# Attention scores as 64-row products in the two halves of the matmul array

## The reference, cut to what matters

```python
Qr = jnp.einsum('bnhd,dr->bnhr', Q, WQr)
Kr = jnp.einsum('bnhd,dr->bnhr', K, WKr)
scores = jnp.einsum('bnhr,bmhr->bnhm', Qr, Kr) / math.sqrt(RANK)   # RANK = 16
A = jax.nn.softmax(scores, axis=-1)
out = jnp.einsum('bnhm,bmhv->bnhv', A, V).reshape(b, n, d)
```

## Time and profile before

| | |
|---|---|
| median of 3 runs | 3451.5 us (3451.04 to 3457.17) |
| profiled execution | 3445.68 us, its span 3443.9 us |
| attention, from its first row tile to the last normalise | 175.1 to 1740.3 us of the span |
| PE busy over the span | 2747.7 us (80%) |
| DVE busy | 2382.6 us (69%) |
| ACT busy | 1604.9 us (47%) |
| row tiles (L678), column tiles (L689), value products (L704) | 2048, 2048, 4096 matmuls |
| maxima on DVE (L608), exponentials on ACT (L594) | 2048 of each |

### The profile page before, as it was taken

The page is one execution under the profiler, slowest core; times in us unless marked ns, Lnnn a source line. Parts: engine busy times, 40 slices in busy tenths (PEclk is TensorE's granted clock), DMA queues, the critical chain, the costliest instruction groups (busy, mean ns, idle before and its releaser), DMA issues. The chain is left out here.

```text
span 3443.9 us, 53771 instructions
## 1 busy us (share of the span) xinstructions
PE 2747.7 (80%) x13598; PEld 1256.8 (36%) x13598; DVE 2382.6 (69%) x4106; ACT 1604.9 (47%) x3030; POOL 1066.2 (31%) x1044
## 2 busy tenths in 40 slices
PE   3899999999999999999974977733367676587772
PEld 2423232332323223333253576621122222446662
DVE  2798888888888888888527912124499998793223
ACT  1327676776767667677731311113444444122110
POOL 1500000000000000000020577752399996036772
PEclk9969999999999999999985989866699989589996
DMA  8400000000000000000002078721133332125887
GB/s 283 134 20 20 21 20 11 20 20 20 20 11 20 20 20 20 11 20 20 1 8 86 23 190 205 197 63 41 41 117 107 102 110 64 47 64 136 214 216 199
DMA packets 184546, 255.14 MB, mean 74 GB/s; under 512 B 26256, under 2 KB 139984, under 8 KB 184272
## 3 DMA queue, kind: packets, MB, share of 16 engines
q1 hardware_dynamic: 140576, 195.81, 18.6%
q0 software_dynamic: 24576, 37.77, 6.2%
q10 hardware_dynamic: 19120, 18.40, 1.6%
HBM read 189.53 MB, written 62.03 MB: 73 GB/s over the span
## 5 line engine op out<-in xcount | busy, mean ns | idle before, releaser
L608 DVE TENSOR_REDUCE att_mx<-att_pR 128x1 f32<-128x512 f32 x2048 | 1271.0, 683 | 196.3 <-PE att_pR L678 193.4
L594 ACT ACTIVATE att_probs<-att_pS 128x512 f32<-128x512 f32 x2048 | 1062.9, 604 | 502.4 <-PE att_pS L689 502.2
L678 PE MATMUL att_pR<-att_ks,att_qs 96*128 96x512 bf16 x2048 | 801.3, 392 | 15.3 <-POOL att_vh L556 14.0
L689 PE MATMUL att_pS<-att_qs,att_ks 98*128 98x512 bf16 x2048 | 781.4, 385 | 26.2 <-issue 20.1
L704 PE MATMUL att_pA<-att_probs,att_vh 128*17 128x512 f32 x4096 | 544.2, 603 | 0.3 <-ACT att_acc_sb L582 0.2
L561 POOL COPY att_vh<-all_v 128x256 f32 (+1 forms) x32 | 12.7, 400 | 1423.3 <-PE att_pA L704 1423.3
L689 PEld LDWEIGHTS att_pS<-att_qs,att_ks 98*128 98x128 bf16 x2048 | 199.2, 98 | 645.1 <-ACT att_probs L594 405.1
L2019 PE MATMUL sc_pY<-sc_hc,all_ident 128*128 128x512 f32 x512 | 275.6, 665 | 121.5 <-DVE sc_hc L1976 104.9
L1903 POOL TENSOR_TENSOR sc_bh<-ssm_du,sc_b 128x1024 f32<-128x1024 f32 x128 | 298.5, 2353 | 15.9 <-DVE sc_hc L1976 10.2
L678 PEld LDWEIGHTS att_pR<-att_ks,att_qs 96*128 96x128 bf16 x2048 | 201.1, 98 | 278.2 <-DVE att_mx L608 140.2
L1966 DVE TENSOR_TENSOR_SCAN sc_bh<-sc_pD,sc_carry,sc_bh 128x512 f32<-128x512 f32 x192 | 232.2, 1260 | 0.0
(11 more groups left out here) (291 smaller groups left out, 3481.3 us busy)
## 6 DMA issues: line engine op xcount, KB each, us to landing
sc_b<-scan_rows SPq DMA_DIRECT2D x128, 256.0 KB, 3.3
expert_sum<-qkv_zeros ACTq DMA_DIRECT2D x4, 4224.0 KB, 28.2
att_qs<-query_parts SPq DMA_DIRECT2D x192, 64.0 KB, 2.1
att_ks<-key_parts SPq DMA_DIRECT2D x192, 64.0 KB, 2.1
f1e_wg<-in_w_gate SPq DMA_DIRECT2D x64, 192.0 KB
f1e_wu<-in_w_up SPq DMA_DIRECT2D x64, 192.0 KB
f1e_wd<-in_w_down SPq DMA_DIRECT2D x64, 192.0 KB
f2e_wg<-in_w_gate SPq DMA_DIRECT2D x64, 192.0 KB
```

Source lines behind the costliest of these rows:

```text
L594: act.activation(probs[:, k % (2 * HALF), :], pS[:, (s + k) % 3, :], ACT.Exp, scale=float(DK) ** -0.5).then_inc(expd, 1)
L608: dve.tensor_reduce(mx4[s][:, k // QC, k % QC:k % QC + 1], pR[:, (s + k) % 3, :], AX.X, ALU.max).then_inc(maxed, 1)
L678: pe.matmul(pR[:, (s + k) % 3, :], qs[s][0:PAIR_ROWS, t * P:(t + 1) * P], ks[s][0:PAIR_ROWS, c * GROUP:(c + 1) * GROUP], start=True, stop= ...
L689: pe.matmul(pS[:, (s + k) % 3, :], ks[s][:, t * P:(t + 1) * P], qs[s][:, c * GROUP:(c + 1) * GROUP], start=True, stop=True).then_inc(col_s ...
```

## The change

All score matmuls now have at most 64 rows, so that they fit in one half (upper 64 or lower 64 rows) of the array.

- The order of the six parts is changed, so that the first 64 rows hold the four products of parts 0 and 1. Row tiles are computed from those alone: the maxima come from two-part scores. The shift only has to be near the true maximum, since it cancels in the division.
- Every row of `qs` and `ks` gets a twin in the other half, in new tiles `q2` and `k2`. Even tiles use the upper half, odd tiles the lower half.
- A column tile is two products into one bank: 64 rows, then the remaining 34 (32 parts and the two shift rows).
- PE's order goes in pairs of steps: column tiles k and k+1 (upper, lower, upper, lower), then row tiles k and k+1. After every second pair there is a half of `values`.
- `pS` has four banks in place of three; the fourth is `pO`'s. `combine` and `turn_maxima` now borrow a place of the ring at step 56 of each head, and the places are numbered so that the ring comes out even. The next user of that place is column tile 59; it waits for `normalise` and `send`.
- `normalise` moves on DVE from the middle of the next head to behind `send`, at that same place.
- SP loads 24 pieces in place of 12 per head and issues four shift DMAs in place of two. POOL sets three more pairs of rows of ones.
- `pR` keeps its three banks, and a row tile k still waits for the maximum of tile k-3.

```diff
-Q_PARTS = (0, 1, 2, 0, 1, 0)
-K_PARTS = (0, 0, 0, 1, 1, 2)
+Q_PARTS = (0, 1, 0, 1, 2, 0)
+K_PARTS = (0, 0, 1, 1, 0, 2)
+MAX_PARTS = 4
+MAX_ROWS = DK * MAX_PARTS
...
+REST_ROWS = ROWS - MAX_ROWS
...
-    LOADS = 2 * len(Q_PARTS)
+    LOADS = 2 * 2 * len(Q_PARTS)
+    SHIFTS = 2 * SHIFT_ROWS
+    RING = 4
+    SIDE = STEPS - HALF
+    LEFT_OUT = (16, 32, 44)
+    PLACES = STEPS + 1 + len(LEFT_OUT)
...
-        pS = m.ps("pS", [P, 3, BANK])
+        pS = m.ps("pS", [P, RING, BANK])
         pA = m.ps("pA", [P, BANK])
-        pO = m.ps("pO", [P, BANK])
...
+        def place(k):
+            return k + sum(k >= left for left in LEFT_OUT) + (k >= SIDE)
+        SIDE_PLACE = place(SIDE) - 1
+        STEP_AT = {place(k): k for k in range(STEPS)}
+        def bank(at):
+            return pS[:, at % RING, :]
...
                     for r, part in enumerate(sel):
                         sp.dma_start(tile[DK * r:DK * r + DK, :],
                                      side[part, bass.ds(v(n * DK), DK), :]).then_inc(qk_in[s], 16)
+                        at = (DK * r + MAX_ROWS) % P
+                        sp.dma_start(twin[at:at + DK, :],
+                                     side[part, bass.ds(v(n * DK), DK), :]).then_inc(qk_in[s], 16)
...
                 pool.memset(ks[s][PAIR_ROWS:ROWS, :], 1.0).then_inc(consts, 1)
-                pool.wait_ge(consts, 8 + 2 * s)
+                pool.wait_ge(consts, 8 + 3 * s)
+                pool.memset(k2[s][PAIR_ROWS - MAX_ROWS:REST_ROWS, :], 1.0).then_inc(consts, 1)
+                pool.wait_ge(consts, 9 + 3 * s)
                 pool.memset(vh[s][:, :, DK:DK + 1], 1.0).then_inc(consts, 1)
...
             def head(n, s, turn, ahead):      # on DVE
                 if ahead >= 1:
-                    maxima(n + 1, s1, range(LEAD, 2 * LEAD))
-                if not start(n):
-                    normalise(n - 1)
-                if ahead >= 1:
-                    maxima(n + 1, s1, range(2 * LEAD, STEPS))
+                    maxima(n + 1, s1, range(LEAD, STEPS))
                     negate(n + 1, s1)
                 if ahead >= 2:
                     maxima(n + 2, s2, range(LEAD // 2))
                 if ahead >= 1:
                     send(n + 1, s1, turn)
+                if not start(n):
+                    normalise(n - 1)
                 if ahead >= 2:
                     maxima(n + 2, s2, range(LEAD // 2, LEAD))
...
+            def free_row(n, s, turn, k, first=False):
                 if k == 0:
                     pe.wait_ge(qk_in[s], v(16 * LOADS * (turn + 1)))
                 if not first:
                     pe.wait_ge(maxed, v(STEPS * n + k - 2))
+            def row_score(n, s, k):
+                q, kk = ((qs[s], ks[s]), (q2[s], k2[s]))[k % 2]
+                rows = (slice(0, MAX_ROWS), slice(MAX_ROWS, 2 * MAX_ROWS))[k % 2]
                 t, c = k // QC, k % QC
+                pe.matmul(pR[:, (s + k) % 3, :], q[rows, t * P:(t + 1) * P],
+                          kk[rows, c * GROUP:(c + 1) * GROUP], start=True, stop=True).then_inc(row_scored, 1)
+            def free_bank(n, at):
+                before, n_before = at - RING, n
+                if before < 0:
+                    if start(n):
+                        return
+                    before, n_before = before + PLACES, n - 1
+                if before == SIDE_PLACE:
+                    if not start(n_before):
+                        pe.wait_ge(normed, v(n_before))
+                    if not (isinstance(n_before, int) and n_before == NH - 1):
+                        pe.wait_ge(nmT_ready, v(n_before + 2))
+                elif before in STEP_AT:
+                    pe.wait_ge(expd, v(STEPS * n_before + STEP_AT[before] + 1))
+                else:
+                    free_bank(n_before, before)
+            def col_half(n, s, k, half):
+                c, t = k % QC, k // QC
+                q, kk = ((qs[s], ks[s]), (q2[s], k2[s]))[(k + half) % 2]
+                at = MAX_ROWS * (k % 2)
+                rows = slice(at, at + (MAX_ROWS, REST_ROWS)[half])
+                mm = pe.matmul(bank(place(k)), kk[rows, t * P:(t + 1) * P],
+                               q[rows, c * GROUP:(c + 1) * GROUP], start=not half, stop=bool(half))
+                if half:
+                    mm.then_inc(col_scored, 1)
...
             def head(n, s, turn, ahead):      # on PE
                 for g in range(GR):
-                    for j in range(HALF):
+                    for j in range(0, HALF, 2):
                         k = HALF * g + j
-                        col_score(n, s, turn, k)
+                        if k == SIDE:
+                            free_bank(n, SIDE_PLACE)
+                            if not start(n):
+                                combine(n - 1)
+                            if ahead >= 1:
+                                turn_maxima(n + 1)
...
+                        free_col(n, s, turn, k)
+                        free_col(n, s, turn, k + 1)
+                        for half in range(2):
+                            col_half(n, s, k, half)
+                            col_half(n, s, k + 1, half)
+                        if rows:
+                            for at in range(2):
+                                free_row(n_r, s_r, turn_r, k_r + at)
+                                row_score(n_r, s_r, k_r + at)
+                        if j % QC == 2:
+                            last_values(n, s, g, j // QC)
```

More of the change, by code:

```diff
@@ L457, in phase_attention @@
         ks = [m.sb(f"ks{s}", [ROWS, SEQ], BF16) for s in range(SLOTS)]
+        q2 = [m.sb(f"q2{s}", [P, SEQ], BF16) for s in range(SLOTS)]
+        k2 = [m.sb(f"k2{s}", [P, SEQ], BF16) for s in range(SLOTS)]
         vh = [m.sb(f"vh{s}", [P, KT, DK + 1]) for s in range(SLOTS)]
@@ L514, in load @@
             def load(n, s):
-                for side, tile, sel in ((q_dram, qs[s], Q_PARTS), (k_dram, ks[s], K_PARTS)):
+                for side, tile, twin, sel in ((q_dram, qs[s], q2[s], Q_PARTS), (k_dram, ks[s], k2[s], K_PARTS)):
                     for r, part in enumerate(sel):
@@ L593, in head @@
                         act.wait_ge(col_scored, v(STEPS * n + k + 1))
-                        act.activation(probs[:, k % (2 * HALF), :], pS[:, (s + k) % 3, :], ACT.Exp,
+                        act.activation(probs[:, k % (2 * HALF), :], bank(place(k)), ACT.Exp,
                                        scale=float(DK) ** -0.5).then_inc(expd, 1)
@@ L683, in col_score, with free_col @@
+            def free_col(n, s, turn, k):
                 if k == 0:
-                    pe.wait_ge(shift_in[s], v(16 * SHIFT_ROWS * (turn + 1)))
-                if not (start(n) and k < 3):
-                    pe.wait_ge(expd, v(STEPS * n + k - 2))
+                    pe.wait_ge(shift_in[s], v(16 * SHIFTS * (turn + 1)))
+                free_bank(n, place(k))
+            def col_half(n, s, k, half):
                 c, t = k % QC, k // QC
-                pe.matmul(pS[:, (s + k) % 3, :], ks[s][:, t * P:(t + 1) * P],
-                          qs[s][:, c * GROUP:(c + 1) * GROUP], start=True, stop=True).then_inc(col_scored, 1)
+                q, kk = ((qs[s], ks[s]), (q2[s], k2[s]))[(k + half) % 2]
[5 more added lines that the diff above has]
+                    mm.then_inc(col_scored, 1)
@@ L708, in values, with combine @@
                     mm.then_inc(summed, 1)
-            def combine(n, last=False):
+            def combine(n):
                 pe.wait_ge(acc_out, v(n + 1))
-                if not start(n):
-                    pe.wait_ge(normed, v(n))
-                if not last:
-                    pe.wait_ge(nmT_ready, v(n + 2))
                 for t in range(GT):
@@ L737, in head @@
                 for g in range(GR):
[L738 removed]
+                    for j in range(0, HALF, 2):
                         k = HALF * g + j
[L740 to L751 removed]
+                        if k == SIDE:
[4 more added lines that the diff above has]
+                                turn_maxima(n + 1)
+                        over = (k + LEAD) // STEPS
+                        rows = ahead >= 1 + over
+                        n_r, s_r, k_r = n + 1 + over, (s + 1 + over) % SLOTS, (k + LEAD) % STEPS
+                        turn_r = turn + (s + 1 + over) // SLOTS
+                        free_col(n, s, turn, k)
[9 more added lines that the diff above has]
+                            last_values(n, s, g, j // QC)
             for k in range(STEPS):
[L754 removed]
+                free_row(0, 0, 0, k, first=(k < 3))
+                row_score(0, 0, k)
             turn_maxima(0)
             for k in range(LEAD):
[L757 removed]
+                free_row(1, 1, 0, k)
+                row_score(1, 1, k)
             heads(pe, head)
@@ L760, in _ @@
                 values(NH - 1, (NH - 1) % SLOTS, GR - 1, half)
-            combine(NH - 1, last=True)
+            pe.wait_ge(normed, NH - 1)
+            combine(NH - 1)
 def phase_attention_out(nc, io, x_sb, a_sb, ident):
```

40 lines of the change are left out of this document (12 added, 28 removed).

## The result

| | before | after |
|---|---|---|
| median of four runs, us | 3451.45 (3451.04 to 3457.17) | 3515.98 (3515.13 to 3524.0) |
| first row tile on PE, us | 175.09 | 181.59 |
| end of attention, us | 1740.3 | 1808.05 |
| one head, us | 46.44 | 48.34 |
| four steps (distance of values), us | 2.83 | 2.91 |

The ratio is 1.0188, interval [1.017, 1.0206]: slower by 64.5 us, against 3521 forecast (+70). The profiled execution is the longest of the four, so its own total (a span of 3522.1, against 3513.3 to 3514.4 in the others) is not compared here, only its stages. Attention ends 67.7 us later in it.

What follows compares the result with a forecast made beforehand. PE set the pace before; afterwards a chain of waits through one row bank was to bound four steps at 2.92 us. 42 + 28 + 5.6 - 6 = +70 us gave a median of 3521, range 3400 to 3590 (own bounds +8 to +118).

Steps and rivals of the forecast that it cites:

- The ring: Four steps of attention: a chain of waits through one row maximum takes 2.92 us, before 2.83; +42 us.
- The unknown latency of the 64-row product: In the four-step chain, 64-row results may come sooner or later: 2.84 to 2.97 us, +2 to +66 us.
- Once per head: Work done once in each head takes 2.0 us in place of 1.1; +28 us over 31 heads.
- Step 56: PE's column tile 58 waits there for normalise: 1.72 us over two normal groups of four steps (5.84).
- The negation's group: DVE's negation after a head's last maximum: the next maximum starts at 3.60, not 3.34; +0.26 us.
- The start: Before attention, three more POOL memsets with their waits put PE's first row tile 5.6 us later.
- The last stage: Last 80 steps, columns alone: four banks give 2.14 us per four steps, before 2.42; -6 us.
- The turn-backs: The hardware loop's turn-backs (2.42 us and a slow clock after it, eight times) stay as before.
- DVE did not set the pace: Rival, 13%: PE's stop in attention is hidden, DVE sets 2.40 us per four steps; -186 us, about 3265.
- half hidden: Case of the rival in which DVE sets attention's pace: PE's stop is hidden by half, 3370 us.
- The halves do work side by side: Rival, 6%, claimed they don't: PE needs 3.71 us per four steps of attention; +430 and the rest, about 3910.
- The clock did not fall: Rival, 5%: PE stops 0.5 of every 2.92 us in attention, the clock falls to half; over +850 us.

Runs made afterwards that it cites:

- the reordered kernel: Changed kernel with row pair first, ACT's drain one place earlier, and step 56 put in another order on PE: 3329.21 us, ratio 0.9654 to the kernel before.

## Why the prediction was right, step by step

**The ring.** Predicted 0.42 + 0.68 + 0.06 + 0.33 + 0.99 + 0.44 = 2.92; measured 0.41 + 0.68 + 0.06 + 0.33 + 0.98 + 0.45 = 2.91. Over 492 groups +37.5 us, for +42. That it is this ring was shown from three sides: one maximum shorter by 0.27 shortens it by 0.27; an earlier first row pair takes the column pair out of it, and it falls by that pair's 0.44; a fourth row bank takes DVE out of it. The unknown latency of the 64-row product turned out to be no different: a pair starts within 0.01 us, and DVE can begin 0.41 after it, for 0.42 with a 96-row tile.

**Once per head.** +1.9 per head was measured, of which 16 x 0.076 = 1.2 is the ring; 1.78 is left once per head, for 2.0 forecast and 1.1 before: +21 us, for +28. Step 56 gave 1.49 and not 1.72: the reciprocal starts 0.20 after the cast and not 0.42, and DVE's next maximum starts before the record of the multiply has ended (969.77, for 969.85), so the last row tile of the pair goes 5.56 after the first row pair (970.50) and not 5.80. The negation's group took 3.19 in place of 2.91, +0.28, for +0.26.

**The start.** PE's first row tile is 6.5 us later; 0.9 of it was there before attention began. 5.6 was forecast and is what is left. POOL releases it.

**The last stage.** Two groups of columns alone take 4.42 us (values at 1776.08 and 1780.50), 2.21 each, for 2.14 forecast and 2.42 before: some -4 us in place of -6. The stage as a whole, with what comes once per head in it, is only 1.2 us shorter (55.6 to 54.5 from the last row tile to the end of attention).

**The turn-backs.** "stay" was wrong. A head with one in it cost 4.4 us more than its neighbours before and 5.25 after, 35 and 42 us in all: +7, and PE's waits there say the same (20.1 and 27.4). It offset what the ring and step 56 fell short of. The sum, 37.5 + 21 + 5.6 - 4 + 7 = +67, is how much later attention ends (67.7, of which 0.9 lay before it); the median moved by 64.5. So the +70 is near the truth partly by luck, because two small errors cancel: the four terms are 9.5 us too large together, and 7 are left out. (Its upper bound is also mis-added: the terms' own bounds give +8 to +112, not +118.)

**The rivals.** DVE did not set the pace (2.91, not 2.40), but it was a change of order away: with the row pair first the group takes 2.475, 0.07 more than DVE needs. That kernel's 3359 (by ratio) is still far from the rival's 3265, and near its "half hidden" 3370 by chance: the stop is hidden almost whole, but 37 us are those 0.07, and some 50 are what comes once per head and the turn-backs beyond what the rival counted. The halves do work side by side: both at 901.75, and 3.35 per group once only the columns are serial (3.71 was worked out for all serial, without a wait left). The clock did not fall in the changed kernel with 0.5 us of stop in each 2.91. It never rose in the kernel with all products in one half, whose PE had no gap; so the rival's argument, that such stops would lower the clock, is not borne out by either run. Longer stops go with a fall: behind the 3.23 us of the turn-back the granted clock is 0.50 from 424 to 430 us.

## What to carry to other kernels

When an edit saves slots on an engine that issues in order, draw the ring through the scarcest bank before counting the slots: the saved time turns into waiting if the product that needs the bank now stands closer behind the one that holds it. The remedy is in the order, and the first thing to try is to issue first what feeds the slower reader. After such an edit, work through the things that happen once per head or once per loop turn again: they were hidden by the old idle time, and here they took back some 50 of 210 us (42 and 6).

## What the hardware showed that was not expected

- With every score product in one half of the array the granted clock stayed at 0.50 through attention, with PE recorded as busy in 200.00 of 200 us. With only the columns in one half it was 1.00 over a whole head, as it was side by side. But behind a turn-back the kernel with the columns in one half stayed at 0.50 for some 17 us (457 to 474), the side-by-side one for some 6 (424 to 430). Why is open; the runs only show that a PE that is recorded as busy without a gap can stay at half the clock.
- A change between 64-row and 98-row products costs 0.10 us each time (0.32 against 0.22 from start to start), and the records show it as neither a wait nor a longer matmul.
- A turn-back of the hardware loop is not a constant of the loop: PE waited at them 20.1 us before, 27.4 after, 18.1 in the reordered kernel, for eight each, and with the slow clock behind them the heads that hold them took 35, 42 and 27 us longer. What in the loop's body sets this was not tested.
